# Experts in blocks of 256 rows against blocks of 256 and, behind them, of 128

## The reference

```python
logits = tokens @ router_w.T
rw, re = top_k(softmax(logits), 2)
rw = rw / max(rw.sum(-1), 1e-12)
out = tokens
for e in range(8):
    h = gelu(tokens @ w1[e] + b1[e])
    y = h @ w2[e] + b2[e]
    out = out + combine[:, e:e+1] * y      # combine holds rw at the chosen experts
```

## Time and profile before

| | us |
|---|---|
| median of 3 timed runs | 8617.51 (8617.44 to 8631.68) |
| profiled execution, whole | 8601.11 |
| its span | 8599.1 |
| PE busy | 6095.3 (71%) |
| DVE busy | 5283.9 (61%) |
| POOL busy | 5273.5 (61%) |
| ACT busy | 3164.7 (37%) |

### The profile page before, as it was taken

One profiled execution on the slowest core, in us unless ns is written; L12 is line 12 of the kernel. 1 busy time (PEld: TensorE's weight loads), 2 busy tenths in 40 slices (PEclk: granted clock), 3 DMA queues, 4 the chain that ended last, 5 costly groups with the idle time before them and its releaser, 6 DMA issues. The chain is left out here.

```text
span 8599.1 us, 116455 instructions
## 1 busy us (share of the span) xinstructions
PE 6095.3 (71%) x29707; PEld 4561.1 (53%) x29707; DVE 5283.9 (61%) x14153; ACT 3164.7 (37%) x9232; POOL 5273.5 (61%) x5183
## 2 busy tenths in 40 slices
PE   6586777773488656556699999965577775673599
PEld 5234555553466334444577777754454553452487
DVE  9757888887654566665544444446677767345544
ACT  1245888886222300000333333312344444222322
POOL 0455666664677677777677777745777772424322
PEclk9798999995699867777698999967789986786699
DMA  5475565562355333333111111116333343563365
GB/s 146 158 248 152 173 173 173 168 175 92 127 171 175 108 101 102 101 101 102 26 28 30 29 27 31 27 21 191 102 105 104 104 96 116 173 209 84 121 199 164
DMA packets 635818, 1017.70 MB, mean 118 GB/s; under 512 B 137670, under 2 KB 438618, under 8 KB 633828
## 3 DMA queue, kind: packets, MB, share of 16 engines
q0 software_dynamic: 243360, 540.20, 23.5%
q1 hardware_dynamic: 391876, 470.73, 17.3%
HBM read 792.58 MB, written 225.75 MB: 118 GB/s over the span
## 5 line engine op out<-in xcount | busy, mean ns | idle before, releaser
L4272 POOL DMA_INDIRECT gat_edges_rows<-gat_table,gat_room x1080 | 1171.2, 1084 | 338.2 <-issue 326.4
L2827 POOL DMA_INDIRECT l_edges_ring<-pairs,first_room x832 | 843.0, 1013 | 505.2 <-issue 240.9
L2389 POOL DMA_INDIRECT l_sum_rows<-l_feats,back_room x832 | 827.5, 995 | 266.2 <-issue 239.5
L2409 PE MATMUL l_sum_o<-l_sum_rows,l_sum_s 128*128 128x256 f32 x1664 | 622.6, 536 | 451.6 <-DVE l_sum_s L2420 216.3
L2878 ACT ACTIVATE l_edges_ring<-l_edges_ring,l_edges_weight 128x64 f32<-128x64 f32 x3328 | 816.5, 336 | 0.0
L2409 PEld LDWEIGHTS l_sum_o<-l_sum_rows,l_sum_s 128*128 128x128 f32 x1664 | 417.1, 266 | 650.2 <-DVE l_sum_s L2420 332.8
L2950 PE MATMUL l_edges_o<-l_edges_ring,l_edges_sf 128*128 128x260 f32 x1664 | 536.5, 428 | 146.8 <-DVE l_acc L3083 140.3
L3893 ACT ACTIVATE m_ffn_ht<-m_ffn_hp,m_ffn_b1t 128x256 f32<-128x256 f32 x592 | 280.1, 473 | 931.0 <-PE m_ffn_hp L3861 930.5
L3861 PE MATMUL m_ffn_hp<-m_ffn_xt,m_ffn_w1b 128*128 128x256 f32 x2368 | 557.5, 390 | 51.2 <-DVE m_ffn_xt L3908 44.1
L3871 PE MATMUL m_ffn_yp<-m_ffn_w2b,m_ffn_ht 128*128 128x256 f32 x2368 | 545.4, 384 | 25.7 <-ACT m_ffn_ht L3893 24.7
L2431 DVE TENSOR_TENSOR l_acc<-l_acc,l_sum_o 128x256 f32 x832 | 350.1, 421 | 345.2 <-PE l_sum_o L2409 257.8
(11 more groups left out here) (868 smaller groups left out, 14838.2 us busy)
## 6 DMA issues: line engine op xcount, KB each, us to landing
sorted_rows<-l_proj_zero SPq DMA_DIRECT2D x44, 1032.0 KB, 5.0
m_ffn_xs<-sorted_rows SPq DMA_DIRECT2D x144, 258.0 KB, 3.5
m_ffn_w1b<-in_L_ffn_w SPq DMA_DIRECT2D x32, 1024.0 KB, 6.0
m_ffn_w2b<-in_L_ffn_w SPq DMA_DIRECT2D x32, 1024.0 KB, 5.7
m_ffn_w1b<-in_L_ffn_W SPq DMA_DIRECT2D x56, 512.0 KB, 4.4
m_ffn_w2b<-in_L_ffn_W SPq DMA_DIRECT2D x56, 512.0 KB, 5.5
m_by_node<-gat_edges_ys SPq DMA_DIRECT2D x96, 256.0 KB
l_proj_taken<-m_by_node SPq DMA_DIRECT2D x28, 768.0 KB, 7.3
```

Of the source, the lines that this page charges most:

```text
L2389: pool.indirect_dma_start(rows[:, slot, j, :], None, table, bass.IndirectOffsetOnAxis(ap=L.src[:, t:t + 1], axis=0)).then_inc(got[slot], 16)
L2409: pe.matmul(o[:, j, 0:D], s4[:, q % S4, j, :], rows[:, slot, j, :], start=True, stop=True).then_inc(out_done, 1)
L2827: pool.indirect_dma_start(rows(q, 0, 2 * D)[:, j, :], None, table, bass.IndirectOffsetOnAxis(ap=L.src[:, t:t + 1], axis=0)).then_inc(got[q ...
L4272: pool.indirect_dma_start(rows[:, slot, j, :], None, table, bass.IndirectOffsetOnAxis(ap=L.src[:, q * B + j:q * B + j + 1], axis=0)).then_ ...
```

## The change

`runs_of` now returns two numbers: full runs of 256 rows, a multiple of four, and half runs of 128 rows that come behind all the full ones. With two choices of 8 experts it was 56 runs and is now 48 full and 9 half; with one choice it was 32 and is now 24 and 8. `table` gives each expert its whole pairs of blocks as full runs (as long as there are any) and the rest as half runs. In `experts` every engine's part looks at `blocks(q)`, 2 or 1, and works on so many rows; `tail=half` makes the half runs straight-line code. Weights and biases are loaded for a half run as for a full one. The three functions without a caller (`route`, `dispatch`, `mixture`) are removed. The diff, cut (of `table` only the new lines stand here; `copy_x`, `find_home` and `finish` are narrowed to `n` blocks in the same way as `activate`, the nine instructions of the third mixture's `finish` too):

```diff
-    runs = (k * N + experts * (S2 - 1)) // S2
-    return runs + runs % 2
+    full = k * N // S2 // 4 * 4
+    half = max(experts, (k * N + experts * (P - 1)) // P - 2 * full)
+    return full, half
...
-        self.runs = runs_of(experts, k)
+        self.full, self.half = runs_of(experts, k)
+        self.runs = self.full + self.half
...
-        self.nt, self.ends, self.ones_e = [sb(n, [1, E]) for n in ("nt", "ends", "ones")]
+        self.nt, self.ends, self.ones_e, self.whole, self.half_ends, self.step, self.begun = [
+            sb(n, [1, E]) for n in ("nt", "ends", "ones", "whole", "half_ends", "step", "begun")]
...
+        A, B = R.full, R.half
+        wide = lambda ap, n: bc(ap, 2, [1, n, E])
+        each = lambda ap, n: bc(ap, 1, [1, n, E])
+        nt, ends, whole, half_ends, step, begun = self.nt, self.ends, self.whole, self.half_ends, self.step, self.begun
+        o = Own(dve, self.own_t, 48).at(0)
...
+        o.then(dve.tensor_scalar(nt, self.sofar[0:1, :], P - 1.0, None, ALU.add))
+        o.then(dve.tensor_copy(self.nti[:], nt))
+        o.then(dve.tensor_scalar(self.nti[:], self.nti[:], 7, None, ALU.logical_shift_right))
+        o.then(dve.tensor_copy(nt, self.nti[:]))
+        o.then(dve.tensor_scalar(self.nti[:], self.nti[:], 1, None, ALU.logical_shift_right))
+        o.then(dve.tensor_copy(whole, self.nti[:]))
+        o.then(dve.tensor_tensor_scan(ends, self.ones_e, whole, 0.0, ALU.mult, ALU.add))
+        o.then(dve.tensor_scalar(ends, ends, float(A), None, ALU.min))
+        o.mark(dve.tensor_copy(whole[:, 0:1], ends[:, 0:1]))
+        o.then(dve.tensor_tensor(whole[:, 1:], ends[:, 1:], ends[:, 0:E - 1], ALU.subtract))
+        o.then(dve.scalar_tensor_tensor(out=nt, in0=whole, scalar=-2.0, in1=nt, op0=ALU.mult, op1=ALU.add))
+        o.mark(dve.tensor_tensor_scan(half_ends, self.ones_e, nt, 0.0, ALU.mult, ALU.add))
+        o.then(dve.memset(step, 0.0))
+        o.then(dve.tensor_tensor(step[:, 0:E - 1], whole[:, 1:], whole[:, 0:E - 1], ALU.subtract))
+        o.then(dve.tensor_scalar(step, step, float(S2), None, ALU.mult))
+        o.mark(dve.scalar_tensor_tensor(out=step, in0=nt, scalar=-float(P), in1=step, op0=ALU.mult, op1=ALU.add))
+        o.mark(dve.tensor_scalar(begun, whole, float(S2), None, ALU.mult))
...
+        o.then(dve.tensor_scalar(self.run_f[:, A:], self.run_f[:, A:], -float(A), None, ALU.add))
+        for lo, n, end, size in ((0, A, ends, whole), (A, B, half_ends, step)):
+            at = slice(lo, lo + n)
+            o.then(dve.tensor_tensor(self.cmp[:, at], wide(self.run_f[:, at], n), each(end, n), ALU.is_ge))
+            o.then(dve.tensor_reduce(self.where[:, at], self.cmp[:, at], AX.X, ALU.add))
+            o.then(dve.tensor_tensor(self.cmp[:, at], self.cmp[:, at], each(size, n), ALU.mult))
+            o.then(dve.tensor_reduce(self.begin[:, at], self.cmp[:, at], AX.X, ALU.add))
+        first, last = slice(0, A), slice(A, A + B)
+        o.then(dve.tensor_tensor(self.begin[:, first], self.run_f[:, first], self.begin[:, first], ALU.subtract))
+        o.mark(dve.tensor_scalar(self.begin[:, first], self.begin[:, first], float(S2), None, ALU.mult))
+        o.then(dve.scalar_tensor_tensor(out=self.begin[:, last], in0=self.run_f[:, last], scalar=float(P),
+                                        in1=self.begin[:, last], op0=ALU.mult, op1=ALU.add))
+        o.then(dve.tensor_scalar(self.begin[:, last], self.begin[:, last], begun[:, 0:1], None, ALU.add))
...
 def experts(nc, core, R, sorted_rows, by_node, w1, b1, w2, b2, act_fn, beside=None, onto=None, also=None):
 
     E, _, HID = w1.shape
     HC = HID // P
-    runs = R.runs
+    runs, full, half = R.runs, R.full, R.half
+    assert full % G4 == 0
+    blocks = lambda q: 2 if not fixed(q) or q < full else 1
+    sent = lambda q, par: full * 16 + (q - par - full) * 8 if fixed(q) and q > full else (q - par) * 16
+    brought = lambda q, slot: full * 8 + (q - slot - full) * 4 + 16 if blocks(q) == 1 else (q - slot) * 8 + 32
     with Phase(nc, f"{R.name}_ffn") as ph:
         xs = ph.sb("xs", [P, 2, 2, ROW])
...
-                    row = q * S2
-                    if R.start is not None:
-                        row = nc.values_load(R.start[0:1, ds(q, 1)], engines=(mybir.EngineType.SP,), min_val=0,
-                                             max_val=E * REGION, skip_runtime_bounds_check_because="clamped on chip")
+                    n = blocks(q)
+                    row = nc.values_load(R.start[0:1, ds(q, 1)], engines=(mybir.EngineType.SP,), min_val=0,
+                                         max_val=E * REGION, skip_runtime_bounds_check_because="clamped on chip")
-                    sp.dma_start(xs[:, par], sorted_rows[ds(row, S2), :].rearrange("(h p) d -> p h d", p=P)
+                    sp.dma_start(xs[:, par, 0:n], sorted_rows[ds(row, n * P), :].rearrange("(h p) d -> p h d", p=P)
...
-                steps(sp, runs, [(0, load)])
+                steps(sp, runs, [(0, load)], tail=half)
...
-                    for h in range(2):
+                    for h in range(blocks(q)):
...
-                    steps(pool, runs, [(0, store)] if onto is None else [(0, gather), (2, store)], unroll=G4)
-                pool.wait_ge(y_out[0], 16 * runs)
-                pool.wait_ge(y_out[1], 16 * runs)
+                    steps(pool, runs, [(0, store)] if onto is None else [(0, gather), (2, store)], unroll=G4,
+                          tail=half)
+                for par in range(2):
+                    pool.wait_ge(y_out[par], 16 * full + 16 * len(range(full + par, runs, 2)))
...
-                    for h in range(2):
+                    for h in range(blocks(q)):
+                    n = blocks(q) * P
...
-                            ins = pe.matmul(hp[:, k % HB, 0:S2], w1b[:, par, c, k * P:(k + 1) * P], xt[:, par, c, :],
+                            ins = pe.matmul(hp[:, k % HB, 0:n], w1b[:, par, c, k * P:(k + 1) * P], xt[:, par, c, 0:n],
...
-                    for h in range(2):
+                    for h in range(blocks(q)):
...
-                    steps(pe, runs, [(0, turn), (1, up), (2, down)])
+                    steps(pe, runs, [(0, turn), (1, up), (2, down)], tail=half)
...
+                    n = blocks(q) * P
-                        act.activation(ht[:, par, k, :], hp[:, k % HB, 0:S2], act_fn,
+                        act.activation(ht[:, par, k, 0:n], hp[:, k % HB, 0:n], act_fn,
-                    steps(act, runs, [(1, activate)])
+                    steps(act, runs, [(1, activate)], tail=half)
...
-                    dve.tensor_copy(xt[:, par], xtp[:, par]).then_inc(xt_ready, 1)
+                    n = blocks(q) * P
+                    dve.tensor_copy(xt[:, par, :, 0:n], xtp[:, par, :, 0:n]).then_inc(xt_ready, 1)
...
```

More of the change, by code:

```diff
@@ L3956, in _ @@
                     return
[L3957 to L3969 removed]
+                steps(dve, runs, [(0, copy_x), (0, find_home), (2, finish)], unroll=G4, lead=4 if onto is None else runs + 2,
+                      tail=half)
 def first_routing(core, experts):
[L3974 removed]
+    runs = sum(runs_of(experts, 2))
     later = core.weight[1][0:1].rearrange("o t k -> o (t k)").bitcast(I32)
```

244 lines of the change are left out of this document (21 added, 223 removed).

## The result

The changed kernel took 8546.15 us (median of 4 runs, 8540.26 to 8555.14) against 8620.44 of the kernel before on the same chip (8617.44 to 8631.68): ratio 0.9912, interval 0.9895 to 0.9930. A second set of five (e9) gave 8542.77 and 0.9918 (0.9905 to 0.9932). The forecast was 8548.0. The profiled execution took 8555.14 us, its span 8553.4.

A forecast was written before the change was run, and what follows sets the result against it. It took POOL to bound the first expert stage and saw three different limits; -9.1 - 50.0 - 5.1 - 3.7 - 1.6 = -69.5 us gave 8531.6 us profiled, 8548.0 us with the 16.4 offset; range 8530 to 8580.

The forecast's parts named there:

- First mixture: First expert stage, limited by POOL: seven result stores fewer at 1.30 us each, -9.1 us.
- Second mixture: Second expert stage: nine half runs at 3.5 us replace eight full runs at 4.57, -5.1 us.
- the drain: End of the second mixture: half an add (0.3) and one store (1.3) less, -1.6 us.
- the ring of rows: Second mixture: SyncE's next row request waits behind the bias load, for the result three runs before; 10.5 / 3 = 3.5 us.
- Third mixture: Third expert stage: eight half runs take 68.4 us instead of 118.4, -50.0 us; its drain another -3.7.
- the loads' 8.7 us a half run: Third mixture: 2.62 MB at 301 GB/s take 8.7 us, above TensorE's 8.1, so loads set the pace.
- The table: 19 more VectorE instructions per mixture, about 4.5 us, covered by POOL's scatters in the third: costed 0.
- The loads decide more: Rival, chance 0.16: third's half runs get only 251 GB/s, second's cost a full run's 4.57; sum -44.8, 8572.7 us.
- The clock falls: Rival, chance 0.05 for both stretches: TensorE at 1.2 GHz in half runs of second and third mixture; sum +3.7, 8621.2 us.
- Nothing is saved: Rival, chance 0.03: a run costs what it did whatever its rows; 8613.0 us.
- SyncE's issue blocks: Rival, chance 0.03: each bias issue in closely spaced half runs stands still 5.71 us; sum +27.6, 8645.1 us.
- The offset: Whole kernel: timed median lies 16.4 us above the profiled execution, carried over unchanged from 8531.6 to 8548.0 us.

The follow-up runs named there:

- e9: The changed kernel run again unedited: 8542.77 us, ratio 0.9918.
- e3: Changed kernel, but half runs of all three mixtures do the TensorE products of a full run: 8607.34 us, ratio 0.9987.
- e1: Changed kernel with blocks of two sizes in the third mixture alone, first and second in their old form: 8567.0 us, ratio 0.9945.
- e8: Changed kernel with blocks of two sizes in the second mixture alone, the others in their old form: 8611.18 us, ratio 0.9994.
- e7: Changed kernel with SyncE asking for rows of run q before weights and bias of run q-1: 8553.01 us.
- e10: Changed kernel with SyncE's order first weights of run q-1, rows of run q, then second weights and bias of run q-1: 8540.71 us, ratio 0.9916.
- e11: e10 with the second mixture's down product one step later and two banks for the first product: 8527.35 us, ratio 0.9899.
- e4: Changed kernel, but half runs load only a corner of each weight matrix and compute with stale weights: 8551.03 us.
- e5: Changed kernel with an extra 1 MB weight transfer, read by nobody, in each half run of the third mixture: 8565.81 us, timed once.
- e2: Changed kernel without half runs: old full runs and table, last 8 runs of second and third mixture as straight-line code: 8618.82 us, ratio 1.0006.
- e6: Changed kernel with 40 more small VectorE instructions at the head of each table: 8547.35 us, ratio 0.9920.

## Why the prediction was right, and where it was not

**First mixture**, -9.1: measured -8.9, and over five old and nine new profiles 586.3 against 576.1. Right, and by its mechanism; e3 keeps it, e1 and e8 lose it. But only 8.0 of the 8.9 come up to POOL's last store (577.4 us behind the stage's start before, 569.4 after); 0.8 come from a shorter DRAIN behind it, of which more below.

**Second mixture**, -5.1 and -1.6 for the drain: measured -8.2. The price of a half run was right, 3.53 against 3.5. Its cause was right only in part. Rows do wait, and with the rows ahead the waits for them vanish (e7). But the half run then stayed at 3.5 us (24.6, 24.4 and 24.5 us for seven in e7, e10 and e11), so the ring of rows was not the only thing that held it, and with small weight loads it fell to 3.2 (e4). I take it that several rounds of transfers have almost one length; no run here shows them one by one. The drain was mis-sized: last up product to last store went from 7.35 to 3.99 us, which holds the shorter products of the last run too.

**Third mixture**, -50.0 and -3.7: measured -53.2, by errors that cancel. In parts, before to after: stage start to up product of the first replaced run 366.4 to 365.2; from there to the last up product 103.8 to 55.2 (-48.5 for seven steps); last up product to last store 23.1 to 12.8 (-10.4, of which 6.9 are the eighth step and 3.5 the drain that I had at 3.7); start of the last store to the end of the span 7.1 to 14.0 (+6.9).

*The term that was mis-sized is the loads' 8.7 us a half run.* TensorE set the pace with 7.85, also below the 8.1 by which I priced it (up took 3.57 from start to start and 3.73 with its tail, not 4.0 and 4.1). I had read 301 GB/s at a share of 0.93 as what the DMA engines can give; the change drew 328 and e5 360. The Trainium skill ("TensorE: Matmul & The Clock Gate", section "Back-to-back issue gap") had led to an estimate of 162 ns a record of 128 columns; measured are 3.57 / 32 = 0.112 us, below even the 145 ns that I took from the earlier trace rows, tail included. A rate seen under a demand is a lower bound of what can be had. The bound that I had beside it, TensorE alone, was the case.

*The term that was missing is the 6.9 us behind the last store.* The last row of POOL and, from the view of the line that ends the block, its sequencer's DRAIN (ns, start in us), before and after:

```profile
8592.00 0.98 POOL L3824 DMA_INDIRECT out_x<-m_ffn_ys,m_ffn_home  x1 [0.30 <-issue]
...
L3772 POOLq DRAIN  x1: 2340/2340/2340, 8594.3 to 8594.3; - x1
```
```profile
8539.43 0.99 POOL L3648 DMA_INDIRECT out_x<-m_ffn_ys,m_ffn_home  x1 [6.83 <-DVE m_ffn_ys L3771]
...
L3597 POOLq DRAIN  x1: 9200/9200/9200, 8541.8 to 8541.8; - x1
```

The spans end at 8599.1 and 8553.4. All ten profiles with half runs in the third mixture have 14.0 to 14.3 us here, the four without 7.1 to 7.4, e2 with its straight-line tail among them. The difference is the DRAIN alone, 9.20 us instead of 2.34; it starts 2.3 us behind the last store in both, and what follows it takes 2.4 us in both.

The same instruction ends the other two mixtures, and there it did not get longer. In the second mixture before, with two stores in every run, it already was 9.20 us (starting at 7669.5, line 3772):

```profile
L3772 POOLq DRAIN  x1: 9203/9203/9203, 7669.5 to 7669.5; - x1
```

Counted by the transfers that POOL issues in the block (stores, gathers, moves), the three DRAINs before were 2.83 us for 424, 9.20 for 112 and 2.34 for 128; after, 2.02 for 417, 8.63 for 105 and 9.20 for 112. Each of the fourteen profiles has the value that belongs to its count, to 0.01 us. So as far as these show, the DRAIN goes with how many transfers POOL has issued, not with single stores or straight-line code. It does not simply grow with their number, and what it waits for stays open. The prediction had nothing for it.

**The table**, 0: right, for a reason that I had only partly. The third mixture's took 7.8 us, 3.4 more than before where I had said 4.5; the cover that I named, 5.8 us, had shrunk to 2.4, yet 10.7 us lie behind the scatter, most of them POOL's DRAIN (e6).

**The rivals.** "The loads decide more" asked for 251 GB/s; the change drew 328. "The clock falls": 1.00 in the third's half runs and in the second's (7642 to 7667 us); it falls only behind the last product of the second. "Nothing is saved": 32 records of the up product took 3.73 us instead of 7.07. "SyncE's issue blocks": bias issues in the half runs took 0.34 to 0.35 us in the second mixture; a long one, 5.5 us, stands only at the third stage's start, as before.

**The offset.** I carried 16.4 us from profiled execution to median. The profile after lay 9 us above its median, so the same offset would have failed for its own execution; the forecast of the median held because it was made by differences of stages. That it lay within 2 us is luck: the change was forecast at -69.5 and measured at -74.3, and the base that I took, 8617.5, was 2.9 under the 8620.4 beside which the changed kernel was timed.

## What to carry to other kernels

Halving a padded block pays where the engine that binds halves its work, and each stage has its own such engine: stores on POOL in the first mixture, product columns in the third. Where rounds of transfers take over, as in the second, half the rows still cost 3.5 of the 4.57 us. Removing one wait from a pipeline whose engines are 90% busy finds the next of nearly the same length (e7, e10); what paid was giving a product one more step between its producer and itself (e11: the 48 full runs took 20.6 us less than in e10, 0.43 each). Look at the sequencers at the end of a block too: POOL's DRAIN was 2 to 9 us there and ate 6.9 of the gain. And compare two traces by the lengths of stages: spans of single executions differed by 25 us in code that no one had touched.

## What the runs showed of the hardware

- The 16 DMA engines moved 360 GB/s over 40 us at a share of 1.04 (e5), against 301 at 0.93; a share near 1 was no sign of a limit, as 328 GB/s at 1.00 delayed TensorE by 0.23 us in 40.
- When they do bind, the small row transfer suffers: five waits of 0.2 to 3.5 us for `xs`, none named for the megabyte loads (e5).
- An fp32 product of 128 columns streams at half the price of one of 256: 0.112 us a record against 6.91 / 32 = 0.216. So the 128 x 128 weight load of each record adds no more than 0.01 us to it (0.216 / 2 = 0.108).
- POOL's DRAIN at the end of a mixture took 2.0 to 9.2 us, and its length repeated to 0.01 us in fourteen profiles for a given number of indirect transfers in the block: 2.34 us for 128, 9.20 for 112, 8.63 for 105.
- The same instructions, some 2000 us of them, ended 12.1 us apart in the profiled executions of before and after (1988.0 and 2000.1 us).
